# Experts' weights through DRAM: one store and eight loads a round in place of eight PE spreads

## What is computed

```python
h = jnp.einsum('btd,pd->btp', x, hasher_w)
sim = jnp.einsum('btp,np->btn', h, keys)
vals, idx = jax.lax.top_k(sim, TOP_K)          # TOP_K = 4 of 32 experts
w = jax.nn.softmax(vals, axis=-1)
out = jnp.zeros_like(x)
for k in range(TOP_K):
    ik = idx[..., k]
    proj = jax.nn.silu(jnp.einsum('btd,btdp->btp', x, values_down[ik]))
    o = jnp.einsum('btp,btpd->btd', proj, values_up[ik])
    out = out + o * w[..., k:k + 1]
return x + out * scale
```

## Time and profile before

| | us |
|---|---|
| median of 3 runs | 302.82 (298.81 to 302.82) |
| the profiled execution | 301.16 |
| its span, first to last instruction | 299.1 |
| PE busy | 278.4 |
| DVE busy | 235.5 |
| ACT busy | 197.6 |
| POOL busy | 130.9 |

### The profile page before, as it was taken

One profiled execution on the slowest core, in us unless ns is written; L12 is line 12 of the kernel. 1 busy time (PEld: TensorE's weight loads), 2 busy tenths in 40 slices (PEclk: granted clock), 3 DMA queues, 4 the chain that ended last, 5 costly groups with the idle time before them and its releaser, 6 DMA issues.

```text
span 299.1 us, 10998 instructions
## 1 busy us (share of the span) xinstructions
PE 278.4 (93%) x4660; PEld 146.7 (49%) x4661; DVE 235.5 (79%) x517; ACT 197.6 (66%) x390; POOL 130.9 (44%) x218
## 2 busy tenths in 40 slices
PE   4969999999999989999999999999999999889992
PEld 2644433444434344444557554445565645367482
DVE  4767899989989978987787799987977864148854
ACT  3652487867776668689864876889656689941620
POOL 8476133110115641137556312189365031885852
PEclk9997999999999999999999999999999999999999
DMA  5565095264051202000403030006100000010011
GB/s 158 154 179 150 9 182 118 40 178 118 2 136 31 79 4 83 4 2 25 139 6 81 4 83 5 1 3 177 24 4 2 6 3 3 2 37 2 2 37 35
DMA packets 18574, 17.27 MB, mean 58 GB/s; under 512 B 6830, under 2 KB 16222, under 8 KB 18526
## 3 DMA queue, kind: packets, MB, share of 16 engines
q1 hardware_dynamic: 17856, 16.39, 21.6%
q10 hardware_dynamic: 670, 0.19, 0.3%
HBM read 12.18 MB, written 4.23 MB: 55 GB/s over the span
## 4 chain that ended last, share of the span: by engine, by line
PE 68%; DVE 12%; DMA 6%; ACT 5%; POOL 4%; issue 3%; SPq 1%; POOLq 0%; DVEq 0%
PE sm_ps L1256 16%; PE st_ps L1256 14%; PE ov_ps L1311 14%; PE mi_ps L1256 6%; PE si_ps L1256 5%; DVE neg_max L947 5%; DMA k_stack<-parts_dram 3%; ACT probs L801 2%; DMA wq_sb<-L_attn_Wq 2%; ACT w_rows L703 1%; PE si_ps L1336 1%; PE mi_ps L1318 1%; PE st_ps L1568 1%; PE sm_ps L1336 1%; PE st_ps L1442 1%
## 5 line engine op out<-in xcount | busy, mean ns | idle before, releaser
L947 DVE TENSOR_REDUCE neg_max<-sm_ps 128x1 f32<-128x512 f32 x256 | 166.4, 685 | 29.2 <-PE sm_ps L1256 24.9
L801 ACT ACTIVATE probs<-st_ps 128x512 f32<-128x512 f32 x256 | 138.2, 610 | 34.0 <-PE st_ps L1256 34.0
L1256 PE MATMUL sm_ps<-k_stack,q_stack 96*32 96x512 bf16 x984 | 97.1, 383 | 3.0 <-DVE neg_max L947 2.1
L1256 PE MATMUL st_ps<-q_stack,k_stack 128*32 128x512 bf16 x1024 | 88.6, 380 | 0.2 <-ACT probs L801 0.2
L1311 PE MATMUL ov_ps<-probs,v_cur 128*32 128x256 f32 x1024 | 76.4, 378 | 0.0
L1256 PEld LDWEIGHTS sm_ps<-k_stack,q_stack 96*32 96x32 bf16 x984 | 26.3, 94 | 50.6 <-DVE neg_max L947 33.9
L533 POOL TENSOR_TENSOR hid<-hid,w_rows 128x512 f32<-128x512 f32 x27 | 34.1, 1278 | 30.7 <-ACT w_rows L703 30.7
L1311 PEld LDWEIGHTS ov_ps<-probs,v_cur 128*32 128x32 f32 x1024 | 31.6, 110 | 22.7 <-ACT probs L801 0.4
L1256 PEld LDWEIGHTS st_ps<-q_stack,k_stack 128*32 128x32 bf16 x1024 | 27.7, 96 | 28.3 <-ACT probs L801 9.1
L1010 DVE SCALAR_TENSOR_TENSOR hid<-tanh_sb,mi_ps 128x512 f32<-128x512 f32 x24 | 16.3, 681 | 15.0 <-ACT tanh_sb L838 15.0
L1256 PE MATMUL mi_ps<-x_t,down_sb 128*32 128x512 f32 x192 | 25.1, 592 | 0.0
(11 more groups left out here) (189 smaller groups left out, 301.2 us busy)
## 6 DMA issues: line engine op xcount, KB each, us to landing
q_stack<-parts_dram SPq DMA_DIRECT2D x16, 288.0 KB
k_stack<-parts_dram SPq DMA_DIRECT2D x48, 96.0 KB
parts_dram<-parts SPq DMA_DIRECT2D x24, 128.0 KB, 2.4
x_sb<-L_attn_x SPq DMA_DIRECT2D x4, 256.0 KB, 4.6
out<-y_out SPq DMA_DIRECT2D x3, 256.0 KB, 2.3
down_sb<-L_ffn_values_down SPq DMA_DIRECT2D x1, 512.0 KB, 5.7
up_sb<-L_ffn_values_up SPq DMA_DIRECT2D x1, 512.0 KB, 7.9
rel_win<-rel_dram SPq DMA_DIRECT2D x1, 256.0 KB, 2.7
```

What stands on the lines that cost most here:

```text
L801: nc.scalar.activation(probs[:, u % 2, j, :], st_ps[:, score_bank(u * J + j), :], ACT.Exp, scale=SCORE_SCALE).then_inc(probs_ready, 1)
L947: nc.vector.tensor_reduce(neg_max[:, g % 2, col:col + 1], sm_ps[:, c % 2, :], AX.X, ALU.max, negate=True).then_inc(max_ready, 1)
L1256: i = nc.tensor.matmul(dst[n * TILE:(n + 1) * TILE], weights[:, n * TILE:(n + 1) * TILE], moving, **flags)
```

## The change

In rounds 1 to 3 the eight spreads on PE and their copies on ACT are gone. PE turns `w_tok` itself, in fp32, into 128 rows (chunk by expert) of 128 tokens; ACT copies them to a new tile `w_cols`. SP stores `w_cols` to a DRAM tensor `w_dram`, expert by expert, waits until the store has landed, and issues eight loads, one for each j, that read each expert's 512 weights 32 times over into 32 partitions of `w_rows[:, j]`. In SP's queue this stands behind shift rows 3 and ahead of the next round's shift rows 0 and slice 2. POOL's weighing waits for the loads, and all eight stand behind the split of the next round's shift rows and a fetch of values. The tail's own weights (sample 3) are made as before.

```diff
-        w_rows = sb("w_rows", [P, FJ, S])
+        w_rows, w_cols = sb("w_rows", [P, FJ, S]), sb("w_cols", [C * NE, P])
+        w_dram = nc.dram_tensor("w_dram", [B - 1, NE, C, P], F32, kind="Internal").ap()
+        w_stored, w_loaded = sem("w_stored"), [sem(f"w_loaded{j}") for j in range(FJ)]
...
-                11: (["wt", "down4"], ["w1"]), 12: (["w0"], ["down5"]), 13: (["w2"], ["down6", "w3"]),
-                14: (["shift0", "w4"], ["down7", "w5"]), 15: (["w6"], ["w7"])}
+                11: (["wt", "down4"], []), 12: ([], ["down5"]), 13: ([], ["down6"]), 14: (["shift0"], ["down7"])}
...
@@ SP, round_
+                if attention and experts:
+                    load_weights(t)
                 if attention and more:
                     load_shift(t + 1, 0)
                     load_slice(t + 1, 2)
...
+            def load_weights(t):
+
+                f = t - 1
+                sp.wait_ge(side_done, job(t, "wt", is_side))
+                sp.dma_start(w_dram[f].rearrange("e c q -> c e q"), w_cols[:]).then_inc(w_stored, 16)
+                sp.wait_ge(w_stored, 16 * t)
+                if f:
+                    sp.wait_ge(weighed, hidden_count(f - 1, FJ - 1))
+                for j in range(FJ):
+                    sp.dma_start(w_rows[:, j, :], bass.AP(w_dram.tensor, (f * NE + j * NJ) * S,
+                                                          [[S, NJ], [0, PD], [1, S]])).then_inc(w_loaded[j], 16)
...
@@ POOL, weigh
-                    pool.wait_ge(side_done, job(t, f"w{j}", is_side))
+                    pool.wait_ge(w_loaded[j], 16 * t)
...
@@ POOL, round_
-                if experts:
-                    split_weights(f)
-                    for j in range(SHIFT_AFTER):
-                        weigh(f, t, j)
                 if attention:
                     if more:
                         split_shift(t + 1, 0)
                         fetch_values(t + 1, 2)
                     if experts:
-                        for j in range(SHIFT_AFTER, FJ):
+                        for j in range(FJ):
                             weigh(f, t, j)
...
@@ ACT, expert_copy
-                    copy(w_t[:], si_bf[0:PARTS * NE, 0:S]).then_inc(side_done, 1)
-                elif name in SPREAD:
-                    j = int(name[1:])
-                    act.wait_ge(side_ready, job(t, name, is_side))
-                    if t > 1:
-                        act.wait_ge(weighed, hidden_count(f - 1, j))
-                    copy(w_rows[:, j], si_ps[:]).then_inc(side_done, 1)
+                    if t == B:
+                        copy(w_t[:], si_bf[0:PARTS * NE, 0:S]).then_inc(side_done, 1)
+                        return
+
+                    if f:
+                        act.wait_ge(w_stored, 16 * f)
+                    copy(w_cols[:], si_ps[:, 0:P]).then_inc(side_done, 1)
...
@@ DVE, share
+                if f:
+                    dve.wait_ge(side_done, job(f, "wt", is_side))
...
@@ PE, misc
-                    pe.wait_ge(w_split, f + 1)
-                    pe.wait_ge(spread_made, PARTS)
+                    if t < B:
+                        pe.wait_ge(dve_step, dve_at(f, "w"))
+                    else:
+                        pe.wait_ge(w_split, 1)
+                        pe.wait_ge(spread_made, PARTS)
                     for c in range(C):
+                        if t < B:
+                            i = nc.tensor.matmul(si_ps[c * NE:(c + 1) * NE, 0:P], w_tok[:, c, :], ident[:],
+                                                 start=True, stop=True)
+                            continue
                         i = tiled_turn(si_bf[0:PARTS * NE, c * P:(c + 1) * P],
                                        w_parts[:, c].rearrange("p i n -> p (i n)"), ident_bf[:])
-                elif name in SPREAD:
-                    pe.wait_ge(side_done, job(t, "wt", is_side))
-                    i = spread_weights(bank[:, :], int(name[1:]))
```

More of the change, by code:

```diff
@@ L167, in bass_postln_attention_product_key_ffn @@
                 8: (["up7"], ["down1"]), 9: (["shift3", "o0"], ["down2"]), 10: ([], ["down3"]),
[2 rows of a table removed]
[1 row of a table added]
         SECOND_JOBS = {0: ([], ["o1"]), 2: (["shift1"], []), 6: (["x1t"], ["sim", "shift2"]), 7: ([], ["down0"]),
                        8: ([], ["down1"]), 9: (["shift3"], ["down2"]), 10: (["o0"], ["down3"]),
[2 rows of a table removed]
+                       11: (["wt"], ["down4"]), 12: ([], ["down5"]), 13: ([], ["down6"]), 14: (["shift0"], ["down7"])}
         LAST_JOBS = {0: (["up0"], ["o1"]), 2: (["up1", "shift1"], ["up2"]), 3: (["up3"], []), 4: (["up4"], []),
@@ L176, in bass_postln_attention_product_key_ffn @@
                      8: ([], ["down1"]), 9: (["shift3", "o0"], ["down2"]), 10: ([], ["down3"]),
[2 rows of a table removed]
+                     11: ([], ["wt", "down4"]), 12: ([], ["down5"]), 13: ([], ["down6"]),
+                     15: (["shift0"], ["down7"])}
         TAIL_JOBS = {0: (["o1"], [f"up{j}" for j in range(FJ)]), 5: ([], ["x1t"]), 6: (["sim"], []), 11: ([], ["wt"])}
         OWN = ("shift0", "shift1", "shift2", "shift3", "o0")
-        SPREAD = tuple(f"w{j}" for j in range(FJ))
-        SIDE = ("o0", "wt", f"up{FJ - 1}") + SPREAD
-        SHIFT_AFTER, NORM_AFTER = 2, 3
+        SIDE = ("o0", "wt", f"up{FJ - 1}")
+        NORM_AFTER = 3
         PLACES = dict(attend=(0, 3), stats_a=(1, 3), stats_b=(4, 0), top=(7, 3), late_y=(8, 3), weights=(9, 1),
@@ L213, in here @@
         def here(n, attention, experts, more, late):
-            if n in SPREAD and not attention:
-                return False
             return (late if n[:2] == "up" else attention if n in OWN else experts) and (more or n != "shift0")
@@ L537, in split_weights @@
                 pool.wait_ge(dve_step, dve_at(f, "w"))
-                if f:
-                    pool.wait_ge(side_ready, job(f, "wt", is_side))
-                    apart(pool)
                 nc.gpsimd.tensor_copy(w_parts[:, :, 0, :], w_tok[:]).then_inc(w_chain, 1)
-                pool.wait_ge(w_chain, f * 3 + 1)
+                pool.wait_ge(w_chain, 1)
                 nc.gpsimd.tensor_sub(w_res[:], w_tok[:], w_parts[:, :, 0, :]).then_inc(w_chain, 1)
-                pool.wait_ge(w_chain, f * 3 + 2)
+                pool.wait_ge(w_chain, 2)
                 nc.gpsimd.tensor_copy(w_parts[:, :, 1, :], w_res[:]).then_inc(w_chain, 1)
-                pool.wait_ge(w_chain, f * 3 + 3)
+                pool.wait_ge(w_chain, 3)
                 nc.gpsimd.tensor_sub(w_parts[:, :, 2, :], w_res[:], w_parts[:, :, 1, :]).then_inc(w_split, 1)
@@ L844, in copies @@
                             shift_copy(*((t, int(name[5:])) if name != "shift0" else (t + 1, 0)))
-                        elif name in ("x1t", "sim", "wt") + SPREAD or name.startswith("down"):
+                        elif name in ("x1t", "sim", "wt") or name.startswith("down"):
                             if here(name, attention, experts, more, late):
```

## The result

| | us |
|---|---|
| median after, 4 runs | 341.96 (341.38 to 343.52) |
| median before, on the same chip | 301.9 (298.81 to 302.82) |
| ratio after / before | 1.1355, 95% interval 1.126 to 1.1451 |
| profiled execution after, its span | 342.14, 340.3 |

The account below looks back on a forecast made before the run. PE was taken as the bound in rounds 1 and 2, ACT in round 3. Profiled 301.2 us plus stalls 14.8 and 14.6, tail 13.3 and clock 3.4 gave 347 us, range 300 to 370 (four engines: 324 to 370).

Parts of the forecast that it names:

- Four engines: In the eight loads and the store, first dimension 4 limits transfers to 4 of 16 DMA engines; chance 0.74.
- Speed of one engine: In the eight loads, each engine moves 20.4 GB/s: 3.2 us a load, 25.7 us for eight.
- The fast end of its range: For the eight loads, 27.3 GB/s per engine from a slice's best quarter microsecond: 19.2 us for eight.
- Slice 2 behind the shift rows: In SP's queue, the next slice needs 2.4 us more and is wanted 3.5 us later: no second stall.
- the tail: After round 3, POOL's weighing of the last such sample waits for load 7 and ends 13.3 us later.
- SP's issuing hides, under 7 us: On SP, issuing nine more DMAs takes under 7 us, within the 11 us before shift row 0 is due.
- Late by 14.8 and 14.6, each counted from its own copy: First scores of rounds 2 and 3 wait for shift rows behind the loads, 14.8 and 14.6 us after today's starts.
- PE's gain in units 11 to 15: In rounds 1 and 2, dropping spreads gains 1.7 us each, swallowed because the shift rows' arrival hangs on the copy.
- The clock: After the stalls of rounds 2 and 3, PE's low clock costs 1.7 us each, 3.4 us (ends 0 and 5.1).
- The sum: Whole kernel: 301.2 + 14.8 + 14.6 + 13.3 + 3.4 = 347 us.
- The first rival: All 16 engines serve the loads, eight take 6.4 us and hide; 297.6 us; chance 0.10.
- The 9.6 us: Before round 2's scores, time left for 2.1 MB of loads if shift rows are to be in time; 218 GB/s decides.

Follow-up runs that it names:

- the two runs whose tail kept the full clock: Changed kernel with round 3 spread by PE as before, 330.03 us; changed kernel with weights stored four times for sixteen-engine loads, 305.44 us.

## Why the prediction was right, and where its terms were off

- *Four engines.* Right: share 0.26 where 0.25 was forecast. The Trainium skill's rule ("DMA: Bandwidth & Descriptors", section "Why a DMA increments its semaphore by 16 and not by 1", the largest number up to 16 that divides both slowest dimensions) agrees with all three points: 0.26, 0.54 and 1.05 for first dimensions 4, 8 and 16.
- *Speed of one engine.* The term that was mis-sized most. The prediction took 20.4 GB/s from the x loads, where all 16 engines ran; four engines alone gave 24.7 each. Eight loads at 2.67 us take 21.4 in place of 25.7, 4.3 less in each of three rounds. In these loads an engine moved less when more of them ran: 24.7 with four, 24.4 with eight, 15.7 with sixteen. The number of engines is not all, since the x loads had 20.4 with sixteen. The Trainium skill's 27 GiB/s (29 GB/s) for one engine ("DMA: Bandwidth & Descriptors", section "Specifications") lies above all of these. The fast end of its range was misread: the quarter microsecond of a slice with 328 GB/s had a share of 0.95, so it is 21.6 for each engine at work and not 27.3, and eight loads at it would take 24.3 us and not 19.2.
- *Slice 2 behind the shift rows.* "No second stall" held, but slice 2 did not stay behind: 268 GB/s moved at 147 to 148, before the last load had landed, where the loads alone moved 99. The share was then 0.82, near the 0.78 of slices alone and not near 1, so the twelve engines of the slice seem to include the four of the loads. That fits the last two weighings of round 1, which came 3.9 and 3.1 us apart in place of 2.67. That is 1.7 us back of the 4.3, so the first lateness is 12.4 in place of 14.8, where the loads' speed alone would have made it 10.5. In the tail no slice comes, and there the whole 4 us show: 9.5 in place of 13.3.
- *SP's issuing hides, under 7 us.* Wrong in size: 12.3 us for eight loads, the shift rows issued only at 141.31. Whether it cost anything is open: the engines would still have had the loads ahead of the shift rows, as the run with the loads in ACT's queue suggests.
- *Late by 14.8 and 14.6, each counted from its own copy.* Right in mechanism, and the two add up, as the table shows. PE's gain in units 11 to 15 was swallowed, as said.
- *The clock.* 3.4 us forecast (ends 0 and 5.1). Measured 2.1 + 2.8 + 2.5 = 7.4. The run with PE kept busy shows the 2.8, and the two runs whose tail kept the full clock show the 2.5; the 2.1 is read from a window (5.9 us at 0.63 lose 2.2). The term was too small because the low clock lasted past the 4 us of the earlier trace rows, and because the tail was left out of the middle value.
- *The sum.* Transfers 35.1 in place of 42.7, clock 7.4 in place of 3.4, and 1.3 us by which this execution came earlier to unit 11: 41.2 in place of 46.1. Those 1.3 us are no gain of the change, since PE's turn of `o_sb` in round 0, which the edit does not touch, already starts 1.6 us earlier (64.79 against 66.36). That the total came so near is luck in part: the transfers were put 7.6 us too high and the clock 4.0 too low. The stated range of 300 to 370 was wide enough for another mechanism as well, so it is the stalls, the share of 0.26 and the two waits of 14 us that bear the prediction out.
- *The price of hidden loads.* The first rival set 297.6 us for loads on 16 engines that hide. With one store of four copies they do hide from the scores, and the time was 302.96: the tail's first step came 2.3 us later, counted from the copy of wt, and not 0.2 earlier, and the two rounds gave 1.6 us (121.10 in place of 122.68 from the first copy to the third) and not 3.4. The 9.6 us that it leaves for the data are 9.8 by its own terms.

## What to carry over

Before a broadcast load is put into a kernel, read its first dimension on both sides: four experts there meant four of sixteen DMA engines, and what stood behind the loads, in SP's queue or on POOL, came late. Writing each row four times, by one store, cost 0.6 us more than writing it once (3.1 us from its issue to that of the loads, in place of 2.5) and 0.3 more in ACT's copy (0.59 in place of 0.28), and at the 251 GB/s of sixteen engines eight loads need 8.4 us in place of 21.4. Moving the slow transfer, in its queue or to another, only moved the stall in both runs that tried it (from the shift rows to POOL's weighings); in the last round, where no next round hides the transfer, the old way was the faster one (299.44 against 302.96 us).

## Not expected of the hardware

- One engine moved 24.7 GB/s with four at work, 24.4 with eight (195 GB/s over eight) and 15.7 with sixteen.
- Reading SBUF rows eight times each gave 10.3 GB/s for each busy engine, reading one DRAM row on all engines 12.2, reading sixteen DRAM rows eight times each 15.7.
- SP was held at its issues while earlier loads were unfinished: the first three of the eight took some 0.5 us each, the last three some 2.5, about as long as a load itself (2.67). The chain of the kernel after has these pieces:

```profile
136.12 2.55 SPq L475
138.71 2.55 SPq L475
```

- A queue is not in order across engines: a slice issued behind the loads moved on engines that these left idle while loads were unfinished (268 GB/s in all, of which four engines can have given 99). The Trainium skill has this in "DMA: Bandwidth & Descriptors", section "Queues, rings and completion order": one queue is a separate ring on each DMA engine.
